# Local attention on one core: two buffers for the rotated q and k, and the spreading of the transposed probabilities moved from ScalarE to VectorE

## The reference

```python
q, k, v = jnp.split(qkv, 3, -1)            # 16 heads of 64, for each of 6 layers
q = l2norm(q) * qs
k = l2norm(k) * ksc
q = q * cos * scale + rotate_half(q) * sin * scale
k = k * cos * inv + rotate_half(k) * sin * inv
...
bk2, bv2 = (look(bk), look(bv))            # windows of 32; a query sees its own window and the one before
sim = jnp.einsum('bhwie,bhwje->bhwij', bq, bk2) * QK_SCALE
sim = jnp.where(mask, -jnp.finfo(sim.dtype).max, sim)
attn = jax.nn.softmax(sim, -1)
out = jnp.einsum('bhwij,bhwje->bhwie', attn, bv2)
```

## Time and profile before

| | |
|---|---|
| median of 3 runs | 2465.32 us (2460.13 to 2469.84) |
| the profiled execution, own time | 2471.35 us |
| its span in the profile | 2469.6 us |
| busy: PE, DVE, ACT, POOL | 2149.8, 1743.1, 1772.7, 1081.1 us |
| of the span | 87%, 71%, 72%, 44% |
| TensorE's mean granted clock | 0.958 of full speed |

### The profile page before, as it was taken

The page is one execution under the profiler, slowest core; times in us unless marked ns, Lnnn a source line. Parts: engine busy times, 40 slices in busy tenths (PEclk is TensorE's granted clock), DMA queues, the critical chain, the costliest instruction groups (busy, mean ns, idle before and its releaser), DMA issues. The chain is left out here.

```text
span 2469.6 us, 65852 instructions
## 1 busy us (share of the span) xinstructions
PE 2149.8 (87%) x26476; PEld 1034.3 (42%) x26476; DVE 1743.1 (71%) x2054; ACT 1772.7 (72%) x2574; POOL 1081.1 (44%) x461
## 2 busy tenths in 40 slices
PE   8689999899998899989999889999998777687787
PEld 3244444444444444444444444444444322222355
DVE  5567777677776777767777677776777489999442
ACT  4578878778787887878878788887887465455533
POOL 0354454454544455444545444544454015566030
PEclk8899999999999999999999999999999989999789
DMA  0322233222332223323233222323222100000001
GB/s 22 108 92 87 83 104 101 84 90 83 104 100 88 92 87 104 96 84 99 81 101 104 81 94 82 109 96 100 87 81 81 31 9 0 0 0 0 19 26 43
DMA packets 102069, 181.01 MB, mean 73 GB/s; under 512 B 15904, under 2 KB 67504, under 8 KB 101680
## 3 DMA queue, kind: packets, MB, share of 16 engines
q1 hardware_dynamic: 101776, 176.83, 22.3%
HBM read 24.73 MB, written 1.05 MB: 10 GB/s over the span
## 5 line engine op out<-in xcount | busy, mean ns | idle before, releaser
L766 POOL TENSOR_TENSOR f_rot<-f_raw,f_tabc 128x1024 f32<-128x1024 f32 x192 | 452.3, 2356 | 745.7 <-DVE f_qk L803 617.3
L795 DVE TENSOR_TENSOR f_shuf<-f_shuf,f_tabs 128x1024 f32<-128x1024 f32 x192 | 397.8, 2072 | 245.1 <-DMA f_shuf<-f_raw 244.7
L770 POOL TENSOR_TENSOR f_rot<-f_rot,f_shuf 128x1024 f32<-128x1024 f32 x192 | 452.6, 2357 | 253.8 <-DVE f_shuf L795 253.8
L491 PE MATMUL f_ps<-f_sq,f_same 64*64 64x256 f32 x3072 | 219.0, 401 | 137.6 <-ACT f_sq L665 137.2
L671 ACT ACTIVATE f_rn<-f_ps 128x1024 f32<-128x1024 f32 x192 | 196.2, 1022 | 146.9 <-PE f_ps L491 146.7
L822 DVE TENSOR_REDUCE f_sum<-f_ps 128x8 f32<-128x512 f32 x192 | 132.8, 692 | 155.1 <-ACT f_ps L716 154.8
L803 DVE SCALAR_TENSOR_TENSOR f_qk<-f_rn,f_rot 128x1024 f32<-128x1024 f32 x192 | 233.7, 1217 | 7.1 <-DMA f_rn<-f_rn 5.1
L491 PEld LDWEIGHTS f_ps<-f_sq,f_same 64*64 64x64 f32 x3072 | 109.9, 135 | 287.9 <-issue 268.9
L480 PE MATMUL f_ps<-y_t,f_wq 128*128 128x512 f32 x384 | 220.2, 656 | 10.3 <-ACT f_rn L671 10.1
L662 ACT ACTIVATE f_raw<-f_ps 128x1024 f32<-128x1024 f32 x192 | 194.5, 1013 | 47.1 <-PE f_ps L481 47.1
L673 ACT ACTIVATE f_rn<-f_rn,k_lift 128x1024 f32<-128x1024 f32 x192 | 220.6, 1149 | 6.3
(11 more groups left out here) (262 smaller groups left out, 3509.9 us busy)
## 6 DMA issues: line engine op xcount, KB each, us to landing
f_shuf<-f_raw SPq DMA_DIRECT2D x384, 256.0 KB, 2.4
f_rn<-f_rn SPq DMA_DIRECT2D x384, 128.0 KB, 2.4
e_w<-in_e_w SPq DMA_DIRECT2D x16, 256.0 KB, 2.8
f_wq<-in_f_wq SPq DMA_DIRECT2D x12, 256.0 KB, 3.0
f_wk<-in_f_wk SPq DMA_DIRECT2D x12, 256.0 KB, 4.0
f_wv<-in_f_wv SPq DMA_DIRECT2D x12, 256.0 KB, 4.1
f_wo<-in_f_wo SPq DMA_DIRECT2D x6, 512.0 KB, 3.6
f_w<-in_f_w SPq DMA_DIRECT2D x6, 341.0 KB, 4.6
```

The costliest lines, as they stand in the source:

```text
L491: mm = pe.matmul(view(ps, CH * b + S * t, [1, S], p0=to, rows=64), same_head[64 * h:64 * h + 64, 64 * h:64 * h + 64], sq[64 * h:64 * h + 6 ...
L766: pool.tensor_tensor(view(rot, 0, [S, 4], [1, S]), view(raw, 0, [S, 4], [1, S]), view(tab_c, 0, [S, 2], [0, 2], [1, S]), ALU.mult).then_in ...
L770: pool.tensor_tensor(rot[:, :], rot[:, :], shuf[:, :], ALU.add).then_inc(sem["rot"], 1)
L795: dve.tensor_tensor(view(shuf, 0, [S, 4], [1, S]), view(shuf, 0, [S, 4], [1, S]), view(tab_s, 0, [S, 2], [0, 2], [1, S]), ALU.mult).then_i ...
```

## The change

`rot` becomes two buffers of the same size, used in turn by even and odd pairs; `straight` then waits only for the `normalise` of the pair two back. `spread` leaves ACT. On DVE it becomes two products with a table `keep` of zeros and ones (one of 7 blocks of 96 columns, one of the last 64) that read PSUM and write `ptz`; it stands at the head of DVE's slot, before the maximum, and works on pair j-2, where ACT's stood at the end of its slot and worked on pair j-1. Its semaphore waits are the same.

```diff
-        raw, sq, shuf, rot = (m.sb(f"f_{n}", 2 * UNIT) for n in ("raw", "sq", "shuf", "rot"))
+        raw, sq, shuf = (m.sb(f"f_{n}", 2 * UNIT) for n in ("raw", "sq", "shuf"))
+        rot = [m.sb(f"f_rot{b}", 2 * UNIT) for b in range(2)]
...
-            def spread(i, j):
-
-
-                need(act, sem["t_mm"], i * 8 + j + 1)
-                need(act, sem["pv_mm"], i * 8 + j)
-                act.activation(view(ptz, 32, [96, 8], [1, 32]), view(ps, 6 * CH + 32, [64, 8], [1, 32]), ACT.Copy)
-                act.activation(view(ptz, 0, [96, 8], [1, 32]), view(ps, 6 * CH, [64, 8], [1, 32]), ACT.Copy,
-                               scale=halves[:, 0:1])
-                act.activation(view(ptz, 64, [96, 7], [1, 32]), view(ps, 6 * CH + 64, [64, 7], [1, 32]), ACT.Copy,
-                               scale=halves[:, 1:2]).then_inc(sem["ptz"], 1)
...
-                if had1:
-                    spread(u1, b1)
...
-                need(pool, sem["qk"], i * 8 + j)
-                pool.tensor_tensor(view(rot, 0, [S, 4], [1, S]), view(raw, 0, [S, 4], [1, S]),
+                need(pool, sem["qk"], i * 8 + j - 1)
+                t = rot[j % 2]
+                pool.tensor_tensor(view(t, 0, [S, 4], [1, S]), view(raw, 0, [S, 4], [1, S]),
                                    view(tab_c, 0, [S, 2], [0, 2], [1, S]), ALU.mult).then_inc(sem["straight"], 1)
...
+            def spread(i, j):
+
+                need(dve, sem["t_mm"], i * 8 + j + 1)
+                need(dve, sem["pv_mm"], i * 8 + j)
+                dve.tensor_tensor(view(ptz, 0, [96, 7], [1, 96]), view(ps, 6 * CH, [64, 7], [1, 96]),
+                                  view(keep, 0, [0, 7], [1, 96]), ALU.mult)
+                dve.tensor_tensor(view(ptz, 7 * 96, [1, 64]), view(ps, 6 * CH + 7 * 64, [1, 64]), keep[:, 0:64],
+                                  ALU.mult).then_inc(sem["ptz"], 1)
...
+                had2, u2, b2 = (run, i, j - 2) if j >= 2 else (before, k, j + 6)
+                if had2:
+                    spread(u2, b2)
                 if run:
                     soft_a(i, j)
```

More of the change, by code:

```diff
@@ L317, in local_attention @@
         same_head, ident = m.sb("f_same", C), m.sb("f_ident", C)
-        mask, halves = m.sb("f_mask", 4 * 64), m.sb("f_halves", 2)
+        mask, keep = m.sb("f_mask", 4 * 64), m.sb("f_keep", 96)
         maskb = m.mem.enter_context(nc.sbuf_tensor("f_maskb", [128, 4 * 64], mybir.dt.bfloat16))
@@ L376, in local_attention @@
                   (same_head[:, :], io["k_same"]), (ident[:, :], io["k_ident"]), (mask[:, :], io["k_mask"]),
-                  (halves[:, :], io["k_halves"])]
+                  (keep[:, :], io["k_keep"])]
         n_const = 16 * len(consts)
@@ L769, in straight @@
                 need(pool, sem["turned"], i * 8 + j + 1)
-                pool.tensor_tensor(rot[:, :], rot[:, :], shuf[:, :], ALU.add).then_inc(sem["rot"], 1)
+                pool.tensor_tensor(t[:, :], t[:, :], shuf[:, :], ALU.add).then_inc(sem["rot"], 1)
             def slot(i, m, j, run, more, before):
@@ L803, in normalise @@
                 dve.scalar_tensor_tensor(out=view(qk[j % 2], 0, [KOFF, 2], [1, UNIT]), in0=view(rn, 0, [UNIT, 2], [1, UNIT]),
-                                         scalar=1e12, in1=view(rot, 0, [UNIT, 2], [1, UNIT]),
+                                         scalar=1e12, in1=view(rot[j % 2], 0, [UNIT, 2], [1, UNIT]),
                                          op0=ALU.min, op1=ALU.mult).then_inc(sem["qk"], 1)
@@ L1643, in constants @@
     lower = (np.arange(128) % 64 < WIN).astype(f)
-    k["k_halves"] = np.stack([lower, 1 - lower], 1)
+    k["k_keep"] = np.repeat(np.stack([lower, np.ones(128, f), 1 - lower], 1), WIN, axis=1)
     k["k_eps"] = np.full((C, 1), LN_EPS, f)
```

## The result

| | before | after |
|---|---|---|
| median of 4 runs each | 2467.58 us (2460.13 to 2470.0) | 2512.42 us (2510.13 to 2517.23) |
| span of the profiled execution | 2469.6 us | 2508.9 us |
| mean granted clock of TensorE | 0.958 | 0.966 |

The change makes the kernel slower: ratio 1.0189, 95% interval 1.0172 to 1.0207. Forecast: 2510 us.

What follows compares the result with a forecast made beforehand. Plain slots were taken as bound by a chain of DVE's softmax with exp, normalisation, POOL's product and rotation. Slot terms summed to +1.9 us a turn, 44 us over 23 turns, giving 2510 us; 8-in-10 range 2466 to 2548.

Steps and rivals of the forecast that it cites:

- The hold moves to the normalisation: Local attention, DVE: POOL's earlier product holds the normalisation instead of the rotation; mean near 2.8 us instead of 1.22.
- The spread on DVE: On DVE's chain between rotation and maximum: 0.95 us a slot, bounds 0.88 to 0.99, no hold by POOL expected.
- Plain slots and slots 2 to 4: Local attention: plain slots 8.54 us; slot 2 +1.21, slot 3 +0.81, slot 4 +0.14.
- Slots 5 to 7: Local attention: slots 5 and 6 together about -0.3 us, through ACT's lighter load; slot 7 about 10.2, +0.28.
- B: Rival: PE's clock falls more often in DVE's longer slots, +1.2 us a turn, 27 us more: 2537; chance 0.12.
- A: Rival: the normalisation is not held beside POOL; about -1.7 us a turn, 40 us: 2425; chance 0.13.
- C: Rival: normalisation still goes first, rotation held as today, spread wholly on top; plain slots 9.1, at most 110 us more; chance 0.03.
- D: Rival: even; the spread costs 0.80, awkward slots gain a little more, 2465 to 2475 us; chance 0.10.

Runs made afterwards that it cites:

- e3: The changed kernel with POOL's cosine product on q alone, 512 of 1024 columns: 2454.77 us, ratio 0.9948 to the kernel before.
- e5: The kernel before (one buffer, spread on ACT) with only the normalisation moved ahead of the softmax sum: 2428.80 us, ratio 0.9844.
- e2: The kernel before with the spread moved to DVE and the one buffer for rot kept: 2579.36 us, ratio 1.0449.
- e1: The kernel before with two buffers for rot alone, the spread staying on ACT: 2467.12 us, ratio 1.0015.
- e6: The kernel before with two buffers for rot and the normalisation ahead of the softmax sum, spread on ACT: 2523.38 us, ratio 1.0231 to before.

## Why the prediction was right

*The hold moves to the normalisation*: right in mechanism and size. It ended 1.08 behind POOL's product, as forecast. The mean of 2337 is below the 2.8 that I gave for it, because it is held in 150 of 192 slots; in the other 42 it goes first or meets no product. The Trainium skill's rule on the page "SBUF — State Buffer", section "SBUF: two separate sides" (whichever starts first has the shared ports for its whole instruction), agrees in both directions: in slot 6 of after L792 started first, took 1.22, and POOL's L755 beside it took 3.03 (1243.03 and 1243.45 in the timeline above).

*The spread on DVE*: 0.90 from its start to the maximum, where I took 0.95 between bounds of 0.88 and 0.99. No hold by POOL showed on it (850 ns in the mean for the large product).

*Plain slots and slots 2 to 4*: 8.54 forecast, 8.55 and 8.63 measured as medians of slots 0 and 1. The terms of slots 2, 3 and 4 are within 0.15 of that turn's lengths: work that was hidden while POOL held the rotation, L868 and the pair L861 of before, now lies open between the normalisation and the rotation.

*Slots 5 to 7*: mis-sized in that turn, in opposite senses, and in slots 5 and 6 the mechanism was wrong. They gained 1.08 instead of 0.3: slot 5 is 8.83 here, where it was 10.32. I had put the gain down to ACT, whose lighter load was to bring slot 6's exp from 14.20 behind the maximum of slot 5 to 13.5. After, it comes at 13.25 or 13.26; but before, it came at 13.26 or 13.27 as well, in nine turns, in which slot 5 was 8.92 to 8.95 long and not 10.3 as in fourteen others. So ACT's relief moved it by nothing, and what the fourteen long turns lost was PE's clock (B below). My turn was of the long kind and does not stand for all. In the fourteen, slots 5 and 6 together went from 21.83 to 20.81 in the mean; in the nine, from 20.85 to 21.62. That all turns together gain 0.30, the forecast's number, is luck. The relief was also smaller than the 1.27 a slot that I added up from ACT's rows: these overlap (in the timeline of the buffer alone L685 ends at 1208.04, and exp behind it starts at 1207.92), and ACT's busy time fell by 182 us, 0.95 a slot. In slot 7 I let the raw copy's shorter wait pay for most of the spread. In that turn it did not: before, the additions of the feed-forward output, L878, started 8.39 behind the maximum; after, they start at 8.26, because the rotation there waits for its DMA. The spread then came on top almost whole, 10.70 against 9.92. The medians over all turns say the same, 10.52 against 9.94; the means hardly differ, since four turns of before have a slot 7 of 11.8 to 14.2.

*The rivals.* A (normalisation not held) is excluded by 2337 ns, and e3 shows that the hold costs what was claimed. B (PE's clock falls more often) went the other way, and that is what slot 5 turned on. Its busy times and mean granted clock before, in that turn and in the next, and after, in that turn (start and end, length, busy us and count of PE, PEld, DVE, ACT and POOL, clock, DMA):

```profile
1210.97:1221.29 10.32, 8.19 (x128) 4.46 (x128) 6.63 (x9) 8.77 (x14) 6.05 (x3) 0.83 0.30 90
1287.77:1296.71 8.94, 6.82 (x128) 3.70 (x128) 6.57 (x8) 7.79 (x14) 4.67 (x3) 1.00 0.28 90
...
1227.58:1236.41 8.83, 7.22 (x129) 3.60 (x127) 7.76 (x10) 6.47 (x9) 4.51 (x3) 1.00 0.29 91
```

Before, the clock of slot 5 is 0.83 of full speed in exactly the fourteen turns in which it is 10.3 long, so for a part of it PE ran at the lower of its two levels, 1.2 GHz; it is 1.00 in the nine in which it is 8.9. (The first turn has no feed-forward work and is left out.) After, it is 1.00 in all. PE had waited 2.13 us ahead of L491 before and 1.60 ahead of L492 after (1231.78 in the timeline above), but the 2.13 stand in the nine turns too, so the wait alone does not tell when the clock falls. The long rows of L491, 1.87 instead of 1.09, are this. In local attention as a whole the clock was 0.98 of full speed before and 0.99 after. Between the first maximum and the last, slot 5 gives back 21 us; all other slots together lose 59, and the 38 are what is left.

C (nothing moves) is in part what slots 6 and 7 do: there the raw copy waits for PE, and the normalisation goes first in 24 and 13 turns, but the rotation behind it is held in only 7 and 11. D (even) needed a spread of 0.80, and it was 0.90.

So 2510 stood on terms that held in slots 0 to 4, plus errors of -0.80 in slots 5 and 6 and +0.50 in slot 7 in that turn, of which 0.30 a turn is left; that they come so near to cancelling is luck. What the prediction did not see is PE's clock in slot 5, and why the two edits stand together: the second buffer alone changes nothing, as PE's scores, a loop over ACT and the held rotation of slot 6 take back what DVE gains, and the spread alone costs 4.5%; together they cost 1.9%.

## What to carry to other kernels

A wait that looks like a plain loss may be what keeps two operations apart that exclude each other: before a buffer is doubled, look at what the released operation will meet, on both engines, and whose chain the meeting lies on. Here the single buffer that cost the rotation its time goes with a kernel that is 1.6% faster (e5) once the normalisation is placed ahead of POOL's product, nearly half of it by PE's clock in slot 5; the second buffer took that gain away and more (e6). What it costs to move work from an engine with slack to the chain of another depends on what else stands there, however busy the first engine looks: the spread, 0.90 from its start to the maximum or 173 us in 192 slots, cost between 116 us (e2) and 45 us (after against e1) in three of the four pairs of the table, and in the fourth the kernel became faster. And a turn picked to stand for all is to be compared with the others first: here two kinds of slot 5 differed by 1.4 us.

## What the runs showed of the hardware that was not expected

That 0.10 us decides over 2.1: in e6 the order of starting alone, POOL first by 0.10, made the normalisation 3.33 long instead of 1.22. A held operation of DVE with two SBUF inputs of 1024 ended 1.08 us behind POOL's in the rotation and in the normalisation alike, so most of its 1.22 runs only once POOL is over. The distance is the same throughout: in the eleven traces, 1363 normalisations and rotations took over 1.4 us, and each of them ended 1.08 or 1.09 behind a product or an addition of POOL that had started ahead of it. DVE's operations with one input in PSUM showed no hold beside POOL: 0.69 for 512 elements, 0.85 for 672, 0.21 for 64, with POOL at work or not.

Of TensorE's clock: in slot 5 of before, 14 of 23 turns have a mean of 0.83 and nine of 1.00, with the same wait of PE ahead of them, and the low ones are 1.4 us longer.
